# Attention with masked maxima on one core: turning the maxima earlier and in f16, a split-f16 projection, constants by VectorE, fewer zero rows

## The reference, cut to what matters

```python
h = _layernorm(x, axis=-1) * (1 + ca) + sa
q, k, v = (split_heads(h @ W + bias) for W, bias in ((Wq, bq), (Wk, bk), (Wv, bv)))
scores = jnp.einsum('bhid,bhjd->bhij', q, k)
bias = rel[..., clip(j - i + 511, 0, 511)]          # rel = q . rel_key
attn = softmax(where(j <= i, (scores + bias) * 0.25, -inf), axis=-1)
x = x + ga * (einsum('bhij,bhjd->bhid', attn, v) @ Wo + bo)
h = _layernorm(x, axis=-1) * (1 + cb) + sb
_, topi = jax.lax.top_k(softmax(h @ gate_w.T + gate_b), 2)
for e in range(8):                                   # three layers per expert
    out = out + cw[..., e:e + 1] * (relu(relu(h @ w1[e] + b1[e]) @ w2[e] + b2[e]) @ w3[e] + b3[e])
x = x + gb * out
```

## Time and profile before

| | us |
|---|---|
| median of three runs | 3905.11 (3901.54 to 3906.79) |
| the profiled execution | 3913.09 |
| its span | 3911.5 |
| PE busy / DVE busy / POOL busy | 3411.8 / 2384.1 / 1270.0 |

### The profile page before, as it was taken

The page is one execution under the profiler, slowest core; times in us unless marked ns, Lnnn a source line. Parts: engine busy times, 40 slices in busy tenths (PEclk is TensorE's granted clock), DMA queues, the critical chain, the costliest instruction groups (busy, mean ns, idle before and its releaser), DMA issues. The chain is left out here.

```text
span 3911.5 us, 164368 instructions
## 1 busy us (share of the span) xinstructions
PE 3411.8 (87%) x72480; PEld 2951.2 (75%) x72480; DVE 2384.1 (61%) x4876; ACT 1407.0 (36%) x1690; POOL 1270.0 (32%) x1501
## 2 busy tenths in 40 slices
PE   6964999999989999999899999989999999189980
PEld 4534888888878888888788888878888888168770
DVE  5853567777256666753566777346567771276774
ACT  1320233344512334354123334522233446155551
POOL 1004433222354332234443322344333211222556
PEclk8986999999989999999899999999999999599995
DMA  3764101000311010003111000131000000544664
GB/s 112 207 169 115 34 24 35 28 26 19 91 55 41 29 37 26 19 29 109 37 39 37 29 19 26 45 97 35 29 29 29 22 13 11 176 128 141 191 181 131
DMA packets 249778, 259.11 MB, mean 66 GB/s; under 512 B 104041, under 2 KB 192333, under 8 KB 248957
## 3 DMA queue, kind: packets, MB, share of 16 engines
q1 hardware_dynamic: 227964, 205.30, 17.9%
q0 software_dynamic: 21120, 43.42, 3.6%
HBM read 151.36 MB, written 95.99 MB: 63 GB/s over the span
## 5 line engine op out<-in xcount | busy, mean ns | idle before, releaser
L887 DVE TENSOR_TENSOR att_acc<-att_pm,att_acc 128x512 f32<-128x512 f32 x1920 | 1267.1, 687 | 542.0 <-PE att_pm L1006 265.3
L967 ACT ACTIVATE att_pt<-att_ps 128x1024 f32<-128x1024 f32 x560 | 573.7, 1025 | 1611.9 <-PE att_ps L998 1603.3
L998 PE MATMUL att_ps<-att_qz,table_z 128*128 128x64 f16 x8960 | 729.7, 194 | 8.9 <-issue 8.8
L995 PE MATMUL att_ps<-att_qx,table_x 68*128 68x64 f16 x8960 | 732.1, 195 | 4.7 <-issue 4.6
L970 ACT ACTIVATE att_pt<-att_ps 128x1024 f32<-128x1024 f32 x528 | 515.3, 1022 | 354.1 <-PE att_ps L1006 351.9
L998 PEld LDWEIGHTS att_ps<-att_qz,table_z 128*128 128x128 f16 x8960 | 621.8, 99 | 8.9 <-issue 8.7
L995 PEld LDWEIGHTS att_ps<-att_qx,table_x 68*128 68x128 f16 x8960 | 619.3, 99 | 8.2 <-issue 7.9
L1088 PE MATMUL att_po<-att_pt,att_vn 128*32 128x128 f32 x17408 | 603.3, 280 | 1.8 <-issue 1.6
L991 PE MATMUL att_ps<-att_qs,att_kn 113*128 113x64 f16 x8960 | 455.5, 194 | 76.5 <-DMA att_qs<-s_m 71.3
L1088 PEld LDWEIGHTS att_po<-att_pt,att_vn 128*32 128x32 f32 x17408 | 452.1, 111 | 88.5 <-issue 73.1
L991 PE MATMUL att_pm<-att_qs,att_kn 113*128 113x64 f16 x8672 | 444.9, 195 | 81.3 <-POOL att_qx L759 46.9
(11 more groups left out here) (209 smaller groups left out, 4073.8 us busy)
## 6 DMA issues: line engine op xcount, KB each, us to landing
att_qe<-s_q SPq DMA_DIRECT2D x256, 128.0 KB
moe_xs<-s_h SPq DMA_DIRECT2D x78, 256.0 KB
s_y<-moe_y SPq DMA_DIRECT2D x78, 256.0 KB
s_v<-prj_vx SPq DMA_DIRECT2D x32, 512.0 KB, 3.9
att_vn<-s_v SPq DMA_DIRECT2D x64, 256.0 KB, 3.5
att_qs<-s_q SPq DMA_DIRECT2D x128, 66.0 KB
prj_x<-in_x POOLq DMA_DIRECT2D x16, 512.0 KB, 4.3
att_kn<-s_k SPq DMA_DIRECT2D x128, 64.0 KB, 2.5
```

Of the source, the lines that this page charges most:

```text
L887: dve.tensor_tensor(held, got, held, ALU.max).then_inc(bank_done, 1)
L967: act.activation(pt[:, k % 2, :, t * 64:t * 64 + 64].rearrange("p h (x c) -> p x h c", x=2), ps[t][:, :, :].rearrange("p x (h c) -> p x h ...
L995: last = pe.matmul(groups[:, :, g], keep["table_x"][:, y:y + P], qx[0:G * D + G, s, x * (XQ // G) + g], start=False, stop=(g == XQ // G - ...
L998: last = pe.matmul(groups[:, :, g], keep["table_z"][:, y:y + P], qz[:, s, x * (XQ // G) + g], start=False, stop=(g == XQ // G - 1), skip_g ...
```

## The change

**Projection.** The loops are written out. The weights and the modulated input are each split into an f16 high part and an f16 rest (`ws`, `hs`), and each product becomes three f16 products. ACT now adds the bias and writes the high part; POOL takes both differences. **Attention.** `acc` is f16, the turn is a matmul of `acc` by an f16 identity, the first maximum is clamped at -60000, the planner puts turns in the first 45% of a block and, for a batch's last block, maxima in the first 40% and the late turns from 50%. The constants are set by DVE, the loads at the start are reordered, and the scatter moves from `turn_h` to `norm`. **Experts.** One spare tile of zeros for all, and the eight region ends of the second half are written at tile 8.

```diff
@@ projection, POOL, ACT, DVE, PE
+                def low_input(it):
+                    pool.wait_ge(h_hi[s], u + 1)
+                    pool.tensor_tensor(hs[:, s, 1], hf[:, s], hs[:, s, 0], ALU.subtract).then_inc(h_lo[s], 1)
+                def low(it, n):
+                    pool.wait_ge(hi_done[n], it + 1)
...
+                    pool.tensor_tensor(lo[:, n, :], qf[:, n, :], hi[:, n, :], ALU.subtract).then_inc(lo_done[n], 1)
+                for it in range(NK):
+                    for n in range(4):
+                        if n == 3 and it + 1 < NK:
+                            low_input(it + 1)
+                        low(it, n)
...
+                    act.activation(hs[:, s, 0], hf[:, s], ACT.Copy).then_inc(h_hi[s], 1)
...
+                    act.activation(qf[:, n, :], qp[n][:, :], ACT.Identity, bias=bias).then_inc(qf_done[n], 1)
...
-                    pe.wait_ge(hT_done[s], u + 1)
+                    pe.wait_ge(h_lo[s], u + 1)
...
+                        for pw, ph in PARTS:
+                            for eh in range(EH):
+                                last = pe.matmul(qp[n][:, :], ws[:, n // 2, pw, eh, ...], hs[:, s, ph, eh, :], ...)
@@ planner
-        end = 0.9 if late else 1.0
+        end = 0.4 if late else 1.0
-        line += [((at + 0.7) / 5.5, 1, at, s) for at, s in enumerate(turning)]
+        line += [((at + 0.7) / 5.5 * 0.45, 1, at, s) for at, s in enumerate(turning)]
-        line += [(2 + at, 1, at, s) for at, s in enumerate(late)]
+        line += [(0.5 + 0.05 * at if n > 0 else 2 + at, 2, at, s) for at, s in enumerate(late)]
@@ attention
-        acc = a.sb("acc", [P, 2, H, P])
+        acc = a.sb("acc", [P, 2, H, P], F16)
...
-                            dve.tensor_copy(held, got).then_inc(bank_done, 1)
+                            dve.tensor_scalar(held, got, LOWEST, None, ALU.max).then_inc(bank_done, 1)
...
-                            last = pe.transpose(full[:, g * P:(g + 1) * P], acc[:, n % 2, 4 * r + g, :], keep["ident"][:, :])
+                            last = pe.matmul(full[:, g * P:(g + 1) * P], acc[:, n % 2, 4 * r + g, :], keep["ident_h"][:, :], ...)
...
+                        sp.wait_ge(spread, 1)
+                        load_qe(2)
+                        sp.wait_ge(m_in[0], 32)
+                        load_kv(0, 3)
...
+                        sp.wait_ge(m_in[1], 32)
+                        sp.wait_ge(cleared, 2)
+                        for j in range(4, NB):
                             load_kv(0, j)
...
+                    if kind == "norm" and n >= RING - 1:
+                        scatter(n + 1 - RING)
...
+                dve.memset(kn[:, 0:4], -1.0)
                 dve.memset(qs[:, :, :, :, :], 0.0).then_inc(cleared, 1)
+                dve.memset(kn[:, 4:], -1.0)
+                dve.memset(kx[:, :, :, :], -1.0).then_inc(cleared, 1)
@@ experts, SP
+                def close_regions(f):
+                    sp.wait_ge(ends_done, 1)
+                    for n in range(f * NX, (f + 1) * NX):
...
+                close_regions(0)
+                sp.wait_ge(zero_out, (NX + 1) * 16)
...
+                    if t == NX:
+                        close_regions(1)
```

More of the change, by code:

```diff
@@ L51 @@
 MASK = 30000.0
+LOWEST = -60000.0
 REL0 = P + W - 1
@@ L283, in phase_project, with order @@
         NK = B * CPB
-        def order(eng, ahead, main):
-            def batch(b, last):
-                for c in range(CPB):
-                    it = b * CPB + c
-                    following = (b, c + 1, it + 1) if c + 1 < CPB else (b + 1, 0, it + 1)
-                    main(b, c, it, None if last and c == CPB - 1 else following)
+        def order(ahead, main):
             ahead(0, 0, 0)
-            with eng.Fori(0, B - 1) as b:
-                batch(b, False)
-            batch(B - 1, True)
+            for it in range(NK):
+                main(it // CPB, it % CPB, it, ((it + 1) // CPB, (it + 1) % CPB, it + 1) if it + 1 < NK else None)
         slot_use = lambda b, c: b * (CPB // 2) + c // 2
@@ L436, in main @@
                     for n in range(2):
-                        pe.wait_ge(vx_done[n], it)
+                        if it:
+                            pe.wait_ge(vx_done[n], it)
                         for j in range(2):
-                            for eh in range(EH):
-                                last = pe.matmul(vp[n][:, j, :], hT[:, s, eh, (2 * n + j) * P:(2 * n + j + 1) * P],
-                                                 wv[:, eh, :], start=(eh == 0), stop=(eh == EH - 1))
+                            for pw, ph in PARTS:
+                                for eh in range(EH):
+                                    last = pe.matmul(vp[n][:, j, :], hs[:, s, ph, eh, (2 * n + j) * P:(2 * n + j + 1) * P],
+                                                     ws[:, 2, pw, eh, :], start=(pw == ph == eh == 0), stop=(ph == 1 and eh == EH - 1))
                         last.then_inc(vp_done[n], 1)
-                order(pe, ahead, main)
+                order(ahead, main)
             @block.sync
@@ L448, in _ @@
                 sp.dma_start(io["s_q"][:, :, 2 * D].rearrange("b u h t -> (b u) (h t)"), nought[:, :]).then_inc(nought_out, 16)
-                with sp.Fori(0, NK) as it:
+                for it in range(NK):
                     for n in range(4):
@@ L824, in bank @@
                         normalise(n)
-                    if kind == "turn_h" and n >= RING - 2:
-                        late = max(n + 3 - NBLK, 0)
-                        for m in range(n + 2 - RING + max(late - 1, 0), n + 3 - RING + late):
-                            scatter(m)
+                    if kind == "norm" and n >= RING - 1:
+                        scatter(n + 1 - RING)
+                    if kind == "turn_h" and n >= NBLK - 2:
+                        scatter(n + 3 - RING)
                 def step(n):
@@ L1030, in bank @@
                         for g in range(4):
-                            last = pe.transpose(full[:, g * P:(g + 1) * P], acc[:, n % 2, 4 * r + g, :], keep["ident"][:, :])
+                            last = pe.matmul(full[:, g * P:(g + 1) * P], acc[:, n % 2, 4 * r + g, :], keep["ident_h"][:, :],
+                                             start=True, stop=True, skip_group_check=True)
                     if kind == "rows":
```

179 lines of the change are left out of this document (90 added, 89 removed).

## The result

| | before | after |
|---|---|---|
| median of the runs | 3903.32 us | 3867.45 us (3858.06 to 3868.38) |
| profiled execution | 3913.09 | 3858.06 |
| its span | 3911.5 | 3856.2 |

The account below looks back on a forecast made before the run. TensorE's instructions were taken to bound attention, 2984.5 of 3911.5 us. The terms 12 - 24 - 46 - 18 - 4 - 46 - 21 = -147 gave 3766, or 3758 us as a median, with a range of 3700 to 3845.

Parts of the forecast that it names:

- the projection: Projection stage: f16 products make TensorE cheaper, but the split input's chain and clock loss make a chunk 13.4 us: +12 us.
- the start of attention: Start of attention, to block 3: reordered loads let the first scores for output start earlier, until block 3's queries: -24 us.
- the experts: Ahead of the experts: fewer zero-row transfers on SyncE's queue, so the first tile's load comes earlier: -21 us.
- The planner's shares and the waits for the row: In attention: earlier rows of maxima and turns, -46 us of waits, -18 of clock loss, -4 at batches' last blocks.
- the turn: In attention: f16 products for f32 transposes save 0.24 us in each of 256 steps; three quarters of 61 taken, -46 us.
- VectorE's root beside GpSimd: In the projection: VectorE's chain stopped for one GpSimd instruction, about 0.8 us per chunk, +12 us, in the range only.
- the 15 x 1.7 = 26 that the sum held for the clock: In the projection: TensorE's 2.1 us pause in every chunk is followed by half clock, costing 1.7 us a chunk.
- The +24: The projection's cost if VectorE and GpSimd exclude each other by the skill's rule, rather than +12 us.
- My sign of being wrong: In attention: TensorE's waits for `att_acc` and `att_mx` grown by more than 15 us would show the forecast wrong.
- rival (2): In attention: VectorE's pace cuts the turn to -15, half the row waits stay (+23): +54, 3812 us; chance 0.15.
- rival (5): In attention: row waits only move to waits for `acc`; with the projection at +36, 3852 us at most; chance 0.03.
- the running maximum in f16 at no cost: In attention: VectorE's running maximum held in f16 costs nothing, 681 us-thousandths (ns) against 687 ns in f32.

Follow-up runs that it names:

- Experiment 2: Changed kernel with ScalarE taking the next chunk's square root before the first product's bias and high part, not behind them: 3827.4 us, ratio 0.9791 to before.
- experiment 3, second version: Changed kernel with GpSimd issuing the load of x first, then the next input's difference, then the products' four: 3732.7 us, ratio 0.9672 to before.
- experiment 6: Changed kernel with the planner's shares of before: 3836.6 us where the changed kernel takes 3764.9, and 3895.7 where it takes 3866.7.
- experiment 5: Changed kernel with the running maximum and its turning in f32 again: 3890.9 us, and 3895.3 when repeated beside the changed kernel's 3866.7.
- experiment 7: Changed kernel with a block's turns spread over 70% of it instead of 45%: 3749.0 us, ratio 0.972 to before.
- best2: best1 with GpSimd's product differences held until VectorE has normalised, ahead of the input's difference, and ScalarE splitting the fourth product before modulating: 3694.4 us, ratio 0.9587.
- best1: Changed kernel with square root first on ScalarE, block 3's queries ahead of the keys, TensorE beginning chunks on the input's high part: 3740.0 us, ratio 0.9694.
- best3: best2 with a block's turns spread over 70% of it instead of 45%: 3749.9 us, ratio 0.9592 to before.

## Why the prediction was wrong, step by step

The spans gained 55 us where 147 were forecast, so 92 are missing: 57 in attention from block 3, 26 in the projection, 7 at the start of attention and 2 ahead of and in the experts. Three terms of the sum failed. The planner's shares and the waits for the row, taken at -68, are worth 29 on the first kind; the turn, at -46, is worth 23 to 29; VectorE's root beside GpSimd, priced at +12 and left out of the sum, cost about 44, while the 15 x 1.7 = 26 that the sum held for the clock mostly fell away.

**The projection, +12 against +38.** The step that failed here is the one that cost VectorE's inverse root beside GpSimd "about 0.8 us later in each chunk, +12 us; it stands in the range, not in the sum". Two things in it were wrong. The price: I counted one GpSimd instruction, but the root is five dependent steps, and in the chunk above two of them met GpSimd, 0.75 us more in one and 2.6 in the other: the second stood until two queued differences had both ended. The turn came 2.9 us late in each chunk, and 15 x 2.9 = 44 us. Experiment 2 took back 40, with the root's earlier place in it, and experiment 3, second version, 32. And the place: the row of before that carried it has 1828 ns beside 193, a factor of nine, for just such a small form; the place for a term with a row and a mechanism is the sum. The rule of the Trainium skill (SBUF — State Buffer, Who interferes with whom) says that the later of the two is stopped for the whole instruction. The trace agrees that VectorE is stopped, with its 2.78 us beside GpSimd's 2.28; but it was held through two instructions and not one, and by the recorded starts it began 0.48 us ahead of them, so the rows don't show that it was the later. The +24 that the prediction gave by this rule was nearer than its +12. The price of a spell at half clock I had right, 1.7 us (experiment 2), but in the changed kernel a spell mostly falls on products off the chain and costs 0.6 in the turn. So a chunk took 14.9 us where I had 13.4: 11.7 and 2.9, with up to 0.6 in the turn, in place of the clock's 1.7. That is 15 x 1.5 = 23 of the 26 us that were missing.

**The start of attention, -24 against -17**, was right in its mechanism: the scores for output began at 350.8, 48.6 us into the stage where I had 46, and maxima of block 3 waited for their queries until 89.3 where I had 82.5. The twelve key blocks took 28.9 us, as forecast. Their loads began 4.3 us later than I had them, behind key block 3, weights and queries that SP had still to load, and from the last key to the maxima it took 3.6 us and not 1.

**The rows of maxima and the shares, -68 in three terms:** the step that failed is the reckoning that time which TensorE no longer waits for the row is time gained. The waits did fall, from 51 to 8.2 us. On the first kind, for which the forecast was made, the shares bring 29 us all the same (experiment 6): TensorE's waits on `att_acc` and `att_mx` together rose from 60 to 81 us, and its whole idle time in this stretch fell by only 14 (167.0 to 152.8; its busy time by 43). My sign of being wrong, more than 15 us there, was met. The term had no price for it. On the second kind these waits fell from 54 to 44, and the shares are worth 72, so there the size was right. Whether the earlier turns or GpSimd's order, which follows from the shares, brings it isn't separated.

**The turn, -46 against -23 to -29** (experiment 5, first kind): the saving per step was right, 0.25 us, and 61 us on TensorE nearly so (55), but I took three quarters of it as real because VectorE idles 542 us before its maxima. What arrives is half of the 55. Those 542 us are an average over the kernel and the wrong number: TensorE waits where turns and maxima are crowded, and the changed planner crowds them. The same crowding shows in experiment 7. Shares and turn together, 29 and 23 to 29, make up the 57 us that attention gained on the first kind. On the second kind the turn wasn't measured; there the shares' 72 leave 20 of the 92.

**The chip.** On the second kind the attention from block 3 gained 92 us, near the forecast of 114; on the first kind 57. One chip's profile could not show me the difference; why it exists is open. The range should have allowed for it. My rival (2) comes near the same loss in attention, 54 us, by half of the row waits staying, which did not happen; what happened is rival (5), that the waits move to `acc`, with the projection's loss on top, and I gave it a chance of 0.03 and 3852 at most, where 3867 was measured. Two unlikely-looking terms were both true and in the same direction.

**Experts, -21 against -19**, and the running maximum in f16 at no cost (687 ns before and after) were right.

## What to carry to other kernels

Before you move work to GpSimd, list every VectorE instruction that will run beside it and has its operands in SBUF, small ones above all: a chain of five steps of 0.2 us can wait behind one GpSimd instruction after another, and a wait that keeps the two apart can be worth more than the overlap (10.56 us a chunk in best2 against 13.3 in best1, with ScalarE's and GpSimd's order changed along with it). Time that an engine no longer waits in one row is gained only if no other row grows; add up its idle time over the stage. When a planner squeezes an engine's work into less than half of a block, average idle time no longer says that there is slack. And a gain of 1% should be measured on more than one chip.

## What the runs showed of the hardware

- A VectorE step on 128x4 elements takes 0.16 us alone and 2.78 beside two GpSimd differences; four scalar forms of 128x256 in f32 take 1.38 alone and 4.91 beside three of them.
- Maxima over a PSUM bank with one operand in SBUF take 687 ns on average with the running maximum in f16 as in f32, while GpSimd works a third of the time beside them.
- Of the chips that ran these kernels, one takes 3909 to 3910 us for before (3903 in the first measurement, whose chip isn't known) and two take 3857 to 3860, and the ratio of the changed kernel differs with it: 0.989 and 0.976 (the latter on one of the two). The best versions are at 0.959: best2 on the second kind, best3 on the first.
